# Four row and feature stages of a graph network rearranged, and one residual sum moved from GpSimd to TensorE's accumulation

## The reference

```python
x = x + L0_gnn(ln(x))   # 4-head attention over 53125 edges
x = x + L0_ffn(ln(x))   # t + sum over the top 2 of 8 experts: share * (gelu(t @ w1 + b1) @ w2 + b2), hidden 256
x = x + L1_gnn(ln(x))   # relu(relu(norm_over_nodes(agg @ W_rel.T + b + t @ W_root.T)) + t)
x = x + L1_ffn(ln(x))   # gelu(t @ W1 + b1), top 1 of 8 second halves, hidden 1024
x = x + L2_gnn(ln(x))   # three attentions, each followed by gelu
x = x + L2_ffn(ln(x))   # normalized again with each expert's gain, top 2 of 8, hidden 1024
x = x + L3_gnn(ln(x))   # relu(norm_over_nodes(two convolutions) + t)
x = x + L3_ffn(ln(x))   # ln(share-weighted sum of two experts over all nodes + t) * gamma + beta
```

## Time and profile before

| | |
|---|---|
| time, median of 3 runs | 5067.8 us (5063.89 to 5067.9) |
| profiled execution | 5068.51 us |
| its span, first to last instruction | 5066.8 us |
| mean granted TensorE clock | 0.892 of full |
| busy: TensorE matmul / weight load | 82% / 71% |
| busy: VectorE / ScalarE / GpSimd | 46% / 37% / 18% |

### The profile page before, as it was taken

The page is one execution under the profiler, slowest core; times in us unless marked ns, Lnnn a source line. Parts: engine busy times, 40 slices in busy tenths (PEclk is TensorE's granted clock), DMA queues, the critical chain, the costliest instruction groups (busy, mean ns, idle before and its releaser), DMA issues. The chain is left out here.

```text
span 5066.8 us, 79325 instructions
## 1 busy us (share of the span) xinstructions
PE 4168.4 (82%) x22693; PEld 3600.8 (71%) x22694; DVE 2338.3 (46%) x4169; ACT 1855.0 (37%) x3203; POOL 924.7 (18%) x921
## 2 busy tenths in 40 slices
PE   2889879946499895959998997996599879899676
PEld 2677769945378654847886886885499768688554
DVE  5455558853410302148976994996411230210423
ACT  1434316623210232426665664665143310110322
POOL 2666645505300102200000000000222200000101
PEclk8788889968899897979998998997699989999788
DMA  3555425523443103322212221221222233133000
GB/s 102 125 121 121 116 59 201 213 84 104 110 156 152 34 13 96 104 61 47 58 36 48 57 49 37 56 58 36 74 71 70 71 134 152 73 148 152 13 19 27
DMA packets 469286, 437.46 MB, mean 86 GB/s; under 512 B 357428, under 2 KB 421641, under 8 KB 456350
## 3 DMA queue, kind: packets, MB, share of 16 engines
q1 hardware_dynamic: 433918, 338.42, 22.4%
q0 software_dynamic: 35232, 97.61, 6.8%
HBM read 341.00 MB, written 94.92 MB: 86 GB/s over the span
## 5 line engine op out<-in xcount | busy, mean ns | idle before, releaser
L2632 PE MATMUL p_acc<-p_H,p_eT 125*125 125x256 f32 x3750 | 823.5, 378 | 0.0
L2632 PEld LDWEIGHTS p_acc<-p_H,p_eT 125*125 125x125 f32 x3750 | 695.2, 187 | 106.0
L1416 PE MATMUL p_acc<-p_message,p_spread 125*125 125x260 f32 x1666 | 431.6, 427 | 30.6 <-issue 30.6
L1163 POOL DMA_INDIRECT p_message<-edge_table,p_index x425 | 403.1, 949 | 193.9 <-issue 122.2
L2113 DVE BATCH_NORM_STATS2 features_stats<-F x60 | 29.2, 486 | 873.8 <-ACT F L2104 872.0
L1416 PEld LDWEIGHTS p_acc<-p_message,p_spread 125*125 125x125 f32 x1666 | 352.5, 213 | 101.9 <-issue 32.5
L1881 ACT ACTIVATE p_hid<-p_up,p_b1s 128x125 f32<-128x125 f32 x764 | 272.2, 365 | 396.1 <-PE p_up L1857 352.6
L1857 PEld LDWEIGHTS p_up<-p_xT,p_w1s 128*128 128x128 f32 x3056 | 373.7, 197 | 53.5 <-issue 33.5
L1857 PE MATMUL p_up<-p_xT,p_w1s 128*128 128x125 f32 x3056 | 381.6, 282 | 34.9 <-issue 12.3
L1865 PE MATMUL p_down<-p_w2s,p_hid 128*125 128x256 f32 x1528 | 358.6, 383 | 7.1 <-ACT p_hid L1881 6.0
L2555 ACT ACTIVATE p_eT<-p_turned 125x500 f32<-125x500 f32 (+1 forms) x525 | 251.2, 540 | 203.3 <-PE p_turned L2625 186.6
(11 more groups left out here) (506 smaller groups left out, 6960.2 us busy)
## 6 DMA issues: line engine op xcount, KB each, us to landing
sums_first<-edge_sums SPq DMA_DIRECT2D x39, 1562.5 KB, 6.8
p_count<-edge_counts SPq DMA_DIRECT2D x375, 152.6 KB
p_second<-edge_sums SPq DMA_DIRECT2D x36, 1562.5 KB, 8.1
edge_sums<-p_sums SPq DMA_DIRECT2D x25, 1562.5 KB, 5.5
edge_counts<-p_total SPq DMA_DIRECT2D x25, 683.6 KB
p_w1s<-in_L_ffn_W SPq DMA_DIRECT2D x16, 1024.0 KB
p_got<-made SPq DMA_DIRECT2D x25, 560.0 KB
p_dst_all<-dst_row SPq DMA_DIRECT2D x25, 531.2 KB, 4.4
```

The costliest lines, as they stand in the source:

```text
L1163: pool.indirect_dma_start(message[:, m, k, :], None, table, bass.IndirectOffsetOnAxis(ap=index[:, m, k:k + 1], axis=0)).then_inc(landed[m] ...
L1416: last = pe.matmul(at, spread[:, k], message[0:P, m, k], start=(k == 0), stop=(k == R_CH - 1))
L2632: last = pe.matmul(acc[:, s, 0:C], eT[:, r % 4, a % 4], H[:, a, 0:C], start=(a == 0), stop=(a == T - 1))
```

## The change

- `normalize`, the four plain calls with XN (`direct`): VectorE writes the tile to XN itself, ScalarE's copy L528 goes, TensorE transposes from XN, and the stores wait for VectorE. VectorE waits for nothing in its loop. In all eight calls TensorE's list is written out.
- `collect_rows`: the add of XN is gone from it. `experts_on_units` of sparse layer 0 does it in one add of 125 x 6400 on VectorE, ahead of its first copy.
- `experts_on_units`: ahead of each unit's wait for the down matmuls ScalarE does a Gelu of one element.
- `finish_features`: GpSimd's add goes. For each block TensorE does two f32 matmuls by the identity into the same PSUM place, one of the block and one of XT.
- `gelu_rows`: ScalarE's list is written out in all three calls. In the third VectorE's list is written out too, and takes the statistics of a tile after the add of the next.
- `add_layer_norm`: the loads of gamma and beta, and GpSimd's add of beta, move ahead into `experts`.

```diff
 normalize
+    direct = XN is not None and not twice
-                    dve.wait_ge(slot_turned, i * GT + k + 1)
-                    if XN is not None:
-                        dve.wait_ge(slot_kept, i * GT + k + 1)
-                    dve.tensor_scalar(slot[:, k], X[:, tile(t), :].rearrange("p a c -> p (a c)"), mean[:, tile(t)], rstd[:, tile(t)],
+                    if direct:
+                        o = XN[:, tile(t), :].rearrange("p a c -> p (a c)")
+                    else:
+                        o = slot[:, k]
...
+                    dve.tensor_scalar(o, X[:, tile(t), :].rearrange("p a c -> p (a c)"), mean[:, tile(t)], rstd[:, tile(t)],
-                    if XN is not None:
+                    if twice:
                         act.wait_ge(slot_ready, i * GT + k + 1)
                         act.activation(XN[...], slot[:, k], ACT.Copy, ...
-            with pe.Fori(0, NG) as i:
-                for k in range(GT):
+            for t in range(T):
+                k = t % GT
...
+                of = XN[:, t] if direct else slot[:, k]
 collect_rows
-                if keep is not None:
-                    dve.wait_ge(used, (i + 3) * (GT * K))
-                    o = X[:, i * GT:(i + 1) * GT]
-                    dve.tensor_tensor(o, o, keep[:, i * GT:(i + 1) * GT], ALU.add).then_inc(kept, 1)
-                    dve.wait_ge(kept, i + 1)
 experts_on_units
+                    act.wait_ge(warmed, v + 1)
+                    act.activation(warm[:], g.ones[0:1, 0:1], ACT.Gelu).then_inc(warmed, 1)
                     act.wait_ge(down_done, v)
...
+            if kept is not None:
+                dve.tensor_tensor(kept[0][:], kept[0][:], kept[1][:], ALU.add).then_inc(kept_added, 1)
             feed(0, first=True)
 experts
+            sp.dma_start(gain[:, 0], gamma.partition_broadcast(P)).then_inc(gained, 16)
+            sp.dma_start(gain[:, 1], beta.partition_broadcast(P)).then_inc(gained, 16)
...
+            pool.wait_ge(gained, 32)
+            pool.tensor_tensor(X[:], X[:], gain[:, 1].unsqueeze(1).to_broadcast([P, T, C]), ALU.add).then_inc(offset_added, 1)
 finish_features
-        @block.gpsimd
-        def _(pool):
-            for i in range(NG):
-                for h in range(KH):
-                    pool.wait_ge(normed, i * KH + h + 1)
-                    o = slot[:, i % 2, h]
-                    pool.tensor_tensor(o, o, XT[:, h, i * GN:(i + 1) * GN], ALU.add).then_inc(joined, 1)
-                pe.wait_ge(joined, (i + 1) * KH)
+                pe.wait_ge(normed, (i + 1) * KH)
-                            last = pe.transpose(turned[:, v % 6, a, h * 128:(h + 1) * 128], slot[:, i % 2, h, (k + a) * P:(k + a + 1) * P], g.ident[:])
+                            at = turned[:, v % 6, a, h * 128:(h + 1) * 128]
+                            pe.matmul(at, slot[:, i % 2, h, (k + a) * P:(k + a + 1) * P], g.ident[:], start=True, stop=False)
+                            last = pe.matmul(at, XT[:, h, nodes(i * GT + k + a)], g.ident[:], start=False, stop=True)
 gelu_rows
-            with act.Fori(0, NG) as i:
+            for i in range(NG):
...
-                with dve.Fori(0, NG) as i:
-                    for k in range(GT):
+                for t in range(T):
+                    dve.wait_ge(raised, t + 1)
+                    o = X[:, t]
+                    dve.tensor_tensor(o, o, slot[:, t % GT], ALU.add).then_inc(slot_turned, 1)
+                    if t > 0:
+                        dve.wait_ge(slot_turned, GT + t)
+                        of_rows.of(dve, X, t - 1)
+                dve.wait_ge(slot_turned, GT + T)
+                of_rows.of(dve, X, T - 1)
 add_layer_norm
-            sp.dma_start(gain[:, 0], gamma.partition_broadcast(P)).then_inc(loaded, 16)
-            sp.dma_start(gain[:, 1], beta.partition_broadcast(P)).then_inc(loaded, 16)
...
-            pool.wait_ge(loaded, 32)
-            pool.tensor_tensor(X[:], X[:], gain[:, 1].unsqueeze(1).to_broadcast([P, T, C]), ALU.add).then_inc(offset_added, 1)
...
-            dve.wait_ge(loaded, 32)
-            dve.wait_ge(offset_added, 1)
```

More of the change, by code:

```diff
@@ L445, in normalize @@
         b = ph.sb("b", [P, T])
-        slot = ph.sb("slot", [P, GT, C])
+        slot = None if direct else ph.sb("slot", [P, GT, C])
         turned = ph.psum("turned", [128, GT, 512])
@@ L536, in _ @@
             pe.sem_inc(slot_turned, GT)
-            with pe.Fori(0, NG) as i:
-                for k in range(GT):
-                    pe.wait_ge(slot_ready, i * GT + k + 1)
-                    pe.wait_ge(kept, i * GT + k + 1)
-                    for h in range(KH):
-                        last = pe.transpose(turned[:, k, h * P:(h + 1) * P], slot[:, k, h * 128:(h + 1) * 128],
-                                            g.ident[0:P, 0:P])
-                    last.then_inc(slot_turned, 1)
+            for t in range(T):
+                k = t % GT
+                pe.wait_ge(slot_ready, t + 1)
+                pe.wait_ge(kept, t + 1)
+                of = XN[:, t] if direct else slot[:, k]
+                for h in range(KH):
+                    last = pe.transpose(turned[:, k, h * P:(h + 1) * P], of[:, h * 128:(h + 1) * 128], g.ident[0:P, 0:P])
+                last.then_inc(slot_turned, 1)
 class ProjectLoads(Ahead):
@@ L1672, in split_rows, with collect_rows @@
     eng.dma_start(out[WIDE:P], in_[WIDE:P]).then_inc(sem, 16)
-def collect_rows(nc, made, weight, K, X, of_rows, keep=None):
+def collect_rows(nc, made, weight, K, X, of_rows):
     with Phase(nc) as ph:
@@ L1707, in _, with experts_on_units @@
                                                  in1=o, op0=ALU.mult, op1=ALU.add).then_inc(used, 1)
[L1708 to L1712 removed]
                 for t in range(GT):
[L1714 to L1715 removed]
+                    dve.wait_ge(used, (i + 3) * (GT * K) - GT + t + 1)
                     of_rows.of(dve, X, i * GT + t)
[L1719 removed]
+def experts_on_units(nc, g, table, stored, made, owner, dest, plan, K, w1, b1, w2, b2, hidden, gain=None, offset=None, kept=None):
     HC = hidden // 128
@@ L1954, in sparse_experts, with experts @@
             place(nc, g, picks, owner, dest, plan)
-        experts_on_units(nc, g, table, stored, made, owner, dest, plan, K, **weights)
-        collect_rows(nc, made, weight, K, X, of_rows, keep=XN if keep else None)
-def experts(nc, g, XT, share, out, of_rows, loads, hidden):
+        experts_on_units(nc, g, table, stored, made, owner, dest, plan, K, kept=(X, XN) if keep else None, **weights)
+        collect_rows(nc, made, weight, K, X, of_rows)
+def experts(nc, g, XT, share, out, of_rows, loads, hidden, gamma, beta, gain, X):
     HC = hidden // 128
@@ L2826, in _, with add_layer_norm @@
             then(dve.tensor_tensor(out[:], out[:], b[:, 0].unsqueeze(1).to_broadcast([P, T, C]), ALU.add))
-def add_layer_norm(nc, g, R, of_rows, gamma, beta, X, result):
+def add_layer_norm(nc, g, R, of_rows, gain, X, result):
     with Phase(nc) as ph:
@@ L2840, in add_layer_norm @@
         b = ph.sb("b", [P, T])
-        gain = ph.sb("gain", [P, 2, C])
-        loaded = ph.sem("loaded")
         step = ph.sem("step")
@@ L3082, in build @@
                 route_biases(nc, g, number, share, d["L3_ffn_b2"], XN, chosen)
-                experts(nc, g, XT, share, XN, mixed, chosen, 2 * C)
-                add_layer_norm(nc, g, XN, mixed, d["L3_ffn_gamma"], d["L3_ffn_beta"], X, result)
+                gain = st.enter_context(nc.sbuf_tensor("norm_gain", [P, 2, C], F32))
+                experts(nc, g, XT, share, XN, mixed, chosen, 2 * C, d["L3_ffn_gamma"], d["L3_ffn_beta"], gain, X)
+                add_layer_norm(nc, g, XN, mixed, gain, X, result)
 def kernel(**inputs):
```

31 lines of the change are left out of this document (18 added, 13 removed).

## The result

The changed kernel takes 5008.2 us (median; 5004.9 to 5012.4, 4 runs) where the kernel before took 5065.9 (5059.5 to 5067.9, 4 runs) beside it on the chip. The ratio is 0.9889, 95% interval 0.9872 to 0.9906. The forecast was 5016, its range 5001 to 5038: right in sign and size, 8 us too high. The profiled execution took 5010.2 us.

What follows compares the result with a forecast made beforehand. No engine was taken to bound the whole kernel, a row of stages between barriers, so each touched stage was costed by itself. The terms summed to -51.8 us: 5068.5 to 5016.7, against the median 5016; range 5001 to 5038.

Steps and rivals of the forecast that it cites:

- Normalize: Four plain normalize calls: without ScalarE's copy each goes from 15.5 to 10.2 us, 21.2 saved in all.
- Nobody waits for them: Normalize: stores to the node table start earlier, and nobody waits for them before the gathered rows, used 84 us later.
- Collect, last stage, third gelu: collect_rows without XN's five adds saves 7.2 us; last stage without the wait for beta 13.8; third gelu_rows, reordered, 5.7.
- The moved add: Start of sparse layer 0: the 6.82 us add fits VectorE's 11.69 us idle time beside the gathers and costs nothing.
- gathers wait: Rival, sparse layer 0: gathers wait for the moved add, first rows up to 6.8 us later, 5023 us; chance 0.09.
- One-element Gelu: Sparse layers: table load taken ahead of the down-matmul wait, 4.5 us saved in layers 1 and 2, 0 in layer 0.
- the step from a unit's cycle to the stage: Sparse layers 1 and 2: 0.3 us off the unit cycle for each of 15 loads was counted as 4.5 saved.
- too dear: Rival: the one-element Gelu could bring a table load in every unit, up to 190 us, 5206 in all; chance 0.02.
- Finish: Two finish_features calls: TensorE's 200 instructions become the bound, 27.7 us instead of 23.1, 9.2 lost in all.
- all high, 2.0 lost: Bound for finish_features: with all of TensorE's instructions at the high clock, 2.0 us lost a call.
- low clock throughout: Rival: TensorE stays at the low clock in finish_features, 18.0 us more a call, 5052 us in all; chance 0.07.
- Gelu with transposes: Two gelu_rows calls with transposes: four of five table loads go, 12.3 us each, 4.3 saved each, 8.6 in all.

Runs made afterwards that it cites:

- experiment 6: The changed kernel without the one-element Gelu in the sparse layers' units; 5012.6 us, one run.
- experiment 12: The changed kernel with fourteen matmuls on the identity ahead of the first true one in finish_features; 5007.2 us, one run.
- experiment 5: The changed kernel with the moved add, still one instruction, set to start only when GpSimd has issued its first three gathers; 5012.2 us, one run.

## Why the prediction was right, by its steps

**Normalize.** Right, -20.7 of -21.2. The stages themselves went down by 5.3 to 5.9 us. The first handed 1.2 us back: at its end SyncE's two store instructions took 1.07 and 0.84 us, before 0.32, and the next stage starts behind them. "Nobody waits for them", as I wrote of the stores, was true of the stored rows and not of the issue, which the barrier waits for.

**Collect, last stage, third gelu.** Right: -6.7 of -7.2; -13.8 of -13.8, with VectorE going from the scales to its multiplies without GpSimd; -6.6 of -5.7, VectorE's starts 0.33 us apart against the forecast's 0.34, the stage 18.4 us against 19.4.

**The moved add.** This term failed: 0 forecast, 3.6 measured. The step was "VectorE adds of two SBUF operands running beside gathers of 0.95 us". The operands of the earlier trace rows are not two SBUF tiles, `raise_of` is in PSUM, and the row doesn't say so; the code does. The rival "gathers wait", to which I gave 0.09, is what happened, at half its price: the first rows came 3.6 us later and not 6.8, above all since GpSimd's wait for landing rows became 2.4 us shorter. The Trainium skill's page "SBUF — State Buffer", section "Who interferes with whom", has a VectorE instruction with two SBUF inputs contending with a GpSimd instruction that reads SBUF, the loser blocked for the whole instruction. The trace agrees, 7.43 us beside 6.82, and 2.11 beside 1.49 when the instruction is shorter; the gathers of 2.29 and 2.72 us beside adds of 0.42 it leaves unexplained. It could be told only at the stage: in the total other terms went the other way.

**One-element Gelu.** The mechanism was right (no cycle of 7.5 us is left, 0.3 each) and the sum too large: -1.3 of -4.5 for layers 1 and 2, and by experiment 6 nothing of it is shown to be the Gelu's. What failed is the step from a unit's cycle to the stage: in between stand the switches, which end when the weights have come. In layer 2 the trace shows it, with a wait of 4.24 us instead of 3.53; in layer 1 what took the gain is open. The rival "too dear" never came near: 42 table loads in the three sparse layers as before, only elsewhere.

**Finish.** Right in mechanism, +9.0 of +9.2, and by luck in the last microsecond: I had 27.7 us against an old stage of 23.1, measured 26.8 and 27.2 against 22.6. TensorE sets the pace, and the clock rose 4.1 and 5.0 us after its first matmul, when 19 and 23 of 200 instructions had started (forecast: 25). My bound "all high, 2.0 lost" is 1.8 by its own terms; experiment 12 measured 2.2. The rival of a low clock throughout had no support.

**Gelu with transposes.** Right, -9.5 of -8.6: 12.0 and 11.5 us where I had 12.3.

**What was in no term.** The attentions of layer 2 are 6.3 us shorter through the granted clock at their start. I had costed each stage alone. With the errors above (+4.1 in all) this and 4.3 us over the other stages make the 6.5 by which the spans' difference exceeded my sum.

## What to carry to other kernels

Where a row is to show that two engines don't disturb each other, look up in the code where each operand lies before it is taken as evidence; a tile's name in a row doesn't tell SBUF from PSUM. A long VectorE instruction with both operands in SBUF, beside GpSimd's gathers, should be cut: five pieces in place of one took the delay from 3.6 to 0.2 us at a cost of 0.3 in the adds. Twenty-five pieces were no better (13.6 us to the first copy against 12.8). Moving an elementwise add from an idle engine to TensorE as f32 matmuls pays only if TensorE has the time: here it had 12.5 us busy in 22.6, and four times the instructions made it the bound even at the high clock.

## What the runs showed of the hardware

VectorE's adds of two SBUF tiles held GpSimd's indirect gathers to 0.8 us behind the add's end, in one instruction of 6.82 us for 7.43; an add or a multiply with one operand in PSUM held none (102 and 94 gathers). A f32 matmul on the identity is two instructions where the transpose of the same block is one: 200 against 50 for two operands in place of one, 0.11 us each at granted clock 1.00 and 0.21 at 0.50. What a stage leaves behind in TensorE's clock can be worth as much as an edit: 17.1 to 23.9 us at the low clock in an attention behind the faster `gelu_rows`, 26.7 to 27.1 behind the slower one, 1 to 5 us of its length. And in experiment 5 GpSimd's queue signalled a semaphore written behind three indirect gathers when the first had run.
